# Two expert-routing stages of a macaron block on one core: gate matmul turned round, totals taken into the rank matmuls, token list and first gather moved forward

## What is computed

```python
x = L0_attn_hidden_states                      # (4, 512, 512) f32: 2048 tokens of width 512
x = x + 0.5 * ffn(layernorm(x))
x = x + attention(layernorm(x))                # 32 heads of width 16, q and k layer-normed, causal, ALiBi
x = x + 0.5 * ffn(layernorm(x))

def ffn(x, W_gate, b_gate, W_e, b_e):          # 8 experts, the same weights in both places
    logits = x @ W_gate + b_gate               # (tokens, 8)
    _, top_idx = jax.lax.top_k(logits, 2)
    y_all = relu(einsum('bsd,edh->bseh', x, W_e) + b_e)
    return take_along_axis(y_all, top_idx[..., None], axis=2).mean(axis=2)
```

## Time and profile before

| | us |
|---|---|
| median of three runs | 1024.22 |
| their range | 1021.04 to 1028.01 |
| the profiled execution, its own time | 1027.31 |
| its span in the trace | 1025.6 |
| mean granted TensorE clock | 0.921 of 2.4 GHz |

### The profile page before, as it was taken

One profiled execution on the slowest core, in us unless ns is written; L12 is line 12 of the kernel. 1 busy time (PEld: TensorE's weight loads), 2 busy tenths in 40 slices (PEclk: granted clock), 3 DMA queues, 4 the chain that ended last, 5 costly groups with the idle time before them and its releaser, 6 DMA issues. The chain is left out here.

```text
span 1025.6 us, 20208 instructions
## 1 busy us (share of the span) xinstructions
PE 873.8 (85%) x6688; PEld 646.5 (63%) x6689; DVE 638.0 (62%) x1296; ACT 444.2 (43%) x818; POOL 353.1 (34%) x342
## 2 busy tenths in 40 slices
PE   4874999992999989769999999999859993799994
PEld 4773888871777767645555555555447872688883
DVE  7955344433988877757777777777246768244441
ACT  3431333332244434527767677777623430233331
POOL 6723677763123222300000000000034420677764
PEclk9995999996999999959999999999979975799997
DMA  9954588762165599464666666562078850477863
GB/s 339 373 194 170 106 149 149 144 120 71 42 194 171 173 222 232 154 178 115 159 136 135 134 131 137 137 147 75 23 237 300 314 196 31 109 145 145 149 130 51
DMA packets 112859, 162.08 MB, mean 158 GB/s; under 512 B 16864, under 2 KB 74336, under 8 KB 112512
## 3 DMA queue, kind: packets, MB, share of 16 engines
q1 hardware_dynamic: 94928, 123.85, 41.5%
q0 software_dynamic: 17856, 37.25, 19.1%
HBM read 97.44 MB, written 67.37 MB: 161 GB/s over the span
## 5 line engine op out<-in xcount | busy, mean ns | idle before, releaser
L829 DVE TENSOR_REDUCE att_part<-att_s_ps 128x2 f32<-128x1024 f32 (+2 forms) x160 | 195.5, 1225 | 60.9 <-PE att_s_ps L677 60.5
L791 ACT ACTIVATE att_prob<-att_st_ps 128x512 f32<-128x512 f32 x320 | 173.7, 595 | 78.7 <-PE att_st_ps L703 78.6
L144 PE MATMUL exp_z_ps<-ex_w_hi,exp_xT_hi 128*128 x312 | 132.1, 423 | 1.3 <-DVE exp_xT_lo L1482 0.7
L146 PE MATMUL exp_z_ps<-ex_w_hi,exp_xT_lo 128*128 x312 | 126.2, 404 | 0.0
L145 PE MATMUL exp_z_ps<-ex_w_lo,exp_xT_hi 128*128 x312 | 125.8, 403 | 0.0
L1482 DVE TENSOR_TENSOR exp_xT_lo<-exp_t_ps,exp_xT_hi 128x512 fp32r<-128x512 f32 x78 | 54.0, 692 | 107.2 <-ACT exp_xT_hi L1468 107.2
L1475 ACT ACTIVATE exp_y<-exp_y 128x512 f32<-128x512 f32 x72 | 45.5, 632 | 168.7 <-DVE exp_y L1494 168.7
L1109 POOL TENSOR_TENSOR ex_w_lo<-ex_w_lo,ex_w_hi 128x1024 fp32r<-128x1024 f32 x32 | 76.2, 2395 | 96.2 <-ACT ex_w_hi L1213 64.9
L716 PE MATMUL att_pv_ps<-att_prob,att_v_sb 128*32 128x256 f32 (+2 forms) x1280 | 101.4, 391 | 1.8 <-ACT att_oT L796 1.8
L1410 POOL DMA_INDIRECT exp_xg<-xn,ex_token_of x78 | 78.1, 1002 | 66.2 <-SPq L1382 38.7
L641 POOL CAST att_m_parts<-att_part 128x28 fp32r<-128x28 f32 x32 | 6.6, 208 | 270.3 <-DVE att_part L833 270.3
(11 more groups left out here) (199 smaller groups left out, 1644.0 us busy)
## 6 DMA issues: line engine op xcount, KB each, us to landing
ex_w_lo<-in_L_ffn_W_e SPq DMA_DIRECT2D x32, 512.0 KB, 5.7
v_vals<-st_vals SPq DMA_DIRECT2D x16, 512.0 KB, 2.8
q_parts<-st_partq SPq DMA_DIRECT2D x32, 256.0 KB, 3.4
k_parts<-st_partk SPq DMA_DIRECT2D x32, 256.0 KB, 3.7
att_v_sb<-v_vals SPq DMA_DIRECT2D x32, 256.0 KB, 3.7
ex_bias<-in_L_attn_hidden_states SPq DMA_DIRECT2D x8, 512.0 KB, 7.8
acc<-ex_bias SPq DMA_DIRECT2D x8, 512.0 KB, 8.6
xn<-route_xn SPq DMA_DIRECT2D x8, 512.0 KB, 5.5
```

The lines of the kernel that those rows point to most:

```text
L144: nc.tensor.matmul(out, x_hi[:, s], w_hi(c), start=(c == 0), stop=False)
L146: last = nc.tensor.matmul(out, x_lo[:, s], w_hi(c), start=False, stop=(c == C - 1))
L791: nc.scalar.activation(prob[n % 2][:, col:col + 512], st_ps[(e + half) % 3][:, :], ACT.Exp).then_inc(exp_done, 1)
L829: nc.vector.tensor_reduce(out, src, X_AXIS, ALU.max, negate=True).then_inc(red_done, 1)
```

## The change

- Gate: W_gate's 128x8 blocks are the weights now and the transposed rows of both tiles of a pair (256 columns) move, four matmuls a pair into a PSUM tile of 8 partitions. xT is one tile for a pair. ACT adds the bias as it copies the 8x256 logits out (`logits_out`), and PE turns them back with two transposes (`turn_logits`). Their order on the queues is in the diff. The logits stay in PSUM, and the DVE step that added the bias is gone.
- Totals: the total is written as the rank of a seventeenth tile, so each ones matmul is 16 columns wider and the 16 small ones are gone.
- Listing: `token_of` is written directly behind `id_ps`, ahead of `expert_of`; `row_of` takes two steps fewer.
- The identity, the six small DMAs with their waits, and gather 0 are now POOL's work in the route stage. The gather waits for `token_done`, the transposes and the stores of xn. The experts' stage starts at gather 1 and waits for no identity.
- W_qkv is staged in the tile of W_out (unused in this stage) and not in `ex.bias`; the experts' bias is loaded ahead of W_qkv's third load. The last two `load_wq` waits on x are gone. ACT takes the last weights (15) one place earlier.

```diff
 class Experts
+        self.rows = m.sb("rows", [P, C, D]) if rows is None else rows
+        self.ident = m.sb("ident", [P, P])
+        self.prime = m.sb("prime", [1, ADD_RING * 16])
...
 route_block
-        w_stage = x
+        w_stage = None if w_qkv is None else [wo_turned[:, 2 * i:2 * i + 2, :] for i in range(2)]
+        xn = [ex.rows[:, 2 * i:2 * i + 2, :] for i in range(2)]
+        xT = m.sb("xT", [P, 2, C * P])
+        logits = g_ps[:, 0:TE].rearrange("p (t e) -> p t e", e=E)
+        lg_ps = route_ps if proj else wq_ps[3]
...
 SP, behind the loop
             store_xn(PAIRS - 1)
+            for i in range(XR):
+                sp.wait_ge(x_stored[i], 16 * (PAIRS // XR))
+            sp.wait_ge(xn_done, TILES)
+            sp.dma_start(ex.bias[:, :], b_e ...).then_inc(ex.bias_loaded, 16)
             if w_qkv is not None:
                 for n in range(2, WQ_PAIRS):
                     load_wq(n)
                 sp.wait_ge(wq_tr, 2 * WQ_PAIRS)
...
 POOL, ahead of the low parts
+            pool.wait_ge(ident_done, 1)
+            for r in range(ADD_RING):
+                nc.gpsimd.dma_start(ex.prime[0:1, r * 16:(r + 1) * 16], ident[0:1, 0:16]).then_inc(ex.added[r], 16)
+            for r in range(ADD_RING):
+                pool.wait_ge(ex.added[r], 16)
 POOL, behind them
+            pool.wait_ge(tr_done, TILES)
+            for par in range(2):
+                pool.wait_ge(xn_stored[par], 16 * (PAIRS // 2))
+            pool.wait_ge(token_done, 1)
+            ex.gather(nc, xn_dram, 0, ex.rows[:, 0, :])
 PE
-            def gate(t):
-                pe.wait_ge(copied, t + 1)
+            def gate(u):
+                pe.wait_ge(copied, 2 * u + 2)
+                at_least(pe, lg_out, u)
                 for c in range(C):
-                    last = nc.tensor.matmul(g_ps[:, t * E:(t + 1) * E], xT[t % 2][:, c * P:(c + 1) * P], g_raw[:, c, :],
+                    last = nc.tensor.matmul(lg_ps[0:E, 0:2 * P], g_raw[:, c, :], xT[:, :, c * P:(c + 1) * P],
                                             start=(c == 0), stop=(c == C - 1))
+            def turn_logits(u):
+                pe.wait_ge(lg_out, u + 1)
+                for k in range(2):
+                    t = 2 * u + k
+                    last = nc.tensor.transpose(g_ps[:, t * E:(t + 1) * E], lgT[:, k * P:(k + 1) * P], ident[0:E, 0:E])
+                last.then_inc(gate_done, 1)
             for u in range(PAIRS + 2):
                 if u >= 2:
-                    gate(2 * u - 4)
-                    gate(2 * u - 3)
+                    gate(u - 2)
...
                     transpose(2 * u - 1)
+                if u >= 2:
+                    turn_logits(u - 2)
...
+            nc.tensor.matmul(total_ps, ones_bf[:, :], both[:, 0:2 * E], start=False, stop=False, skip_group_check=True)
             for s in range(1, TILES):
-                last = nc.tensor.matmul(rank_ps[:, s * 2 * E:TE2], ones_bf[:, :], both[:, 0:TE2 - s * 2 * E], start=False,
-            for s in range(TILES):
-                last = nc.tensor.matmul(total_ps, ones_bf[:, :], both[:, s * 2 * E:(s + 1) * 2 * E],
+                last = nc.tensor.matmul(route_ps[:, s * 2 * E:TE2 + 2 * E], ones_bf[:, :], both[:, 0:TE2 - (s - 1) * 2 * E],
 ACT
             def copy(t):
-                at_least(act, gate_done, t - 1)
+                at_least(act, lg_done, t // 2)
+            def logits_out(u):
+                act.wait_ge(lg_done, u + 1)
+                at_least(act, gate_done, u)
+                nc.scalar.activation(lgT, lg_ps[0:E, 0:2 * P], ACT.Identity, bias=bg[:, 0:1]).then_inc(lg_out, 1)
...
                     o_split(2 * u + 3)
+                if u >= 2:
+                    logits_out(u - 2)
                 if u >= 1:
                     copy(2 * u - 2)
                     copy(2 * u - 1)
-                if u < PAIRS - 1:
+                if u < PAIRS:
                     weights(2 * u + 1)
-            weights(TILES - 1)
+            logits_out(PAIRS - 1)
 DVE, behind the 32 one-hots
+            dve.wait_ge(ids_done, 2 * TILES)
+            chain(nc.vector.tensor_copy(found[:, :, :], ids))
+            nc.vector.scalar_tensor_tensor(ex.token_of[:, :], found[:, 2, :], float(P), found[:, 1, :],
+                                           ALU.mult, ALU.add).then_inc(token_done, 1)
             chain(nc.vector.tensor_tensor(past[:, :, :], ends[0:1, :] ...
...
 expert_block, POOL
-            gather(0)
-            make_identity(nc, pool, ident, zeroed, ident_done)
             for s in range(1, AHEAD):
                 gather(s)
-            pool.wait_ge(ident_done, 1)
-            for r in range(RING):
-                nc.gpsimd.dma_start(prime[0:1, r * 16:(r + 1) * 16], ident[0:1, 0:16]).then_inc(added[r], 16)
-            for r in range(RING):
-                pool.wait_ge(added[r], 16)
```

More of the change, by code:

```diff
@@ L865, with __init__ @@
 class Experts:
-    def __init__(self, nc, ctx, prefix):
+    def __init__(self, nc, ctx, prefix, rows=None):
         m = Memory(nc, ctx, prefix)
+        self.rows = m.sb("rows", [P, C, D]) if rows is None else rows
+        self.ident = m.sb("ident", [P, P])
+        self.prime = m.sb("prime", [1, ADD_RING * 16])
+        self.gathered = [m.sem(f"gathered{i}") for i in range(ADD_RING)]
+        self.added = [m.sem(f"added{i}") for i in range(ADD_RING)]
         self.w_hi = m.sb("w_hi", [P, E * C, D], F32R)
@@ L881, in __init__, with gather @@
         self.bias_loaded = m.sem("bias_loaded")
+    def gather(self, nc, xn_dram, s, xg):
+        nc.gpsimd.indirect_dma_start(out=xg, out_offset=None, in_=xn_dram[:, :],
+                                     in_offset=bass.IndirectOffsetOnAxis(ap=self.token_of[:, s:s + 1], axis=0)
+                                     ).then_inc(self.gathered[s % ADD_RING], 16)
 def ring_loop(engine, step, total, ring, first):
@@ L954, in route_block @@
         rest = work[:, TE:2 * TE].rearrange("p (t e) -> p t e", e=E)
+        logits = g_ps[:, 0:TE].rearrange("p (t e) -> p t e", e=E)
+        lg_ps = route_ps if proj else wq_ps[3]
+        lgT = work[0:E, 0:2 * P]
+        root = m.sb("root", [P, 4])[:, :] if proj else route_ps[:, 0:4]
         slot_e = work[:, :].rearrange("p (t k e) -> p t k e", k=2, e=E)
@@ L1076, in _ @@
                 sp.wait_ge(wq_tr, 2 * WQ_PAIRS)
-            for i in range(XR):
-                sp.wait_ge(x_stored[i], 16 * (PAIRS // XR))
-            sp.wait_ge(xn_done, TILES)
-            sp.dma_start(ex.bias[:, :], b_e.rearrange("(a e) h -> a (e h)", a=1).to_broadcast([P, E * D])).then_inc(ex.bias_loaded, 16)
-            sp.wait_ge(bias_loaded, 16)
             for par in range(2):
@@ L1294, in _ @@
             dve.wait_ge(const_done, 12)
-            dve.wait_ge(bias_loaded, 16)
-            dve.wait_ge(gate_done, TILES)
+            dve.wait_ge(gate_done, PAIRS)
             three = [P, TILES, E]
-            chain(nc.vector.tensor_tensor(logits[:, :, :], g_ps[:, 0:TE].rearrange("p (t e) -> p t e", e=E),
-                                          bg_bc[:, :].rearrange("p (a e) -> p a e", a=1).to_broadcast(three), ALU.add))
             for k, source in enumerate((logits, rest)):
@@ L1385, in expert_block @@
         AHEAD = RING - 1
-        ident = m.sb("ident", [P, P])
-        xg = [m.sb(f"xg{i}", [P, D]) for i in range(RING)]
+        ident = ex.ident
+        xg = [ex.rows[:, i, :] if i < C else m.sb(f"xg{i}", [P, D])[:, :] for i in range(RING)]
         xT_hi = [m.sb(f"xT_hi{i}", [P, C * P], F32R) for i in range(2)]
@@ L1393, in expert_block @@
         z_ps = [m.ps(f"z_ps{i}") for i in range(2)]
-        zeroed, ident_done = m.sem("zeroed"), m.sem("ident_done")
-        gathered = [m.sem(f"gathered{i}") for i in range(RING)]
-        added = [m.sem(f"added{i}") for i in range(RING)]
+        gathered, added = ex.gathered, ex.added
         tr_done, hi_done, lo_done, z_done, zb_done, y_done = (
```

57 lines of the change are left out of this document (24 added, 33 removed).

## The result

The changed kernel takes 1031.62 us in the median of 20 runs (1029.01 to 1035.55), the kernel before 1026.43 in the median of 20. The ratio is 1.0044, with a 95% interval of 1.0027 to 1.0062. So the change costs 4.5 us by the ratio (2.8 to 6.4) and 5.2 by the medians, where the forecast had a gain of 5.6; 1031.62 lies above the range's end of 1027.5. Of the 13.0 us between 1031.62 and the forecast's 1018.6, 2.2 come from its base, the median of three runs (1024.22 for 1026.43). The profiled execution took 1029.65 us, with a span of 1027.9.

What follows compares the result with a forecast made beforehand. Bound by the engine-to-engine routing chain, and by PE in route 2's loop. Route 1 (0 - 0.3 - 4.0) and route 2 (+2.5 - 1.3 - 0.3 - 2.2) gave -5.6 us: 1018.6 from 1024.22, range 1009.5 to 1027.5.

Steps and rivals of the forecast that it cites:

- Gate, what is new on the path: Gate start, route 2's loop: waiting for both copies behind `logits_out` starts it 0.8 to 0.9 us later; +4.7 us over six gates.
- The six small DMAs move to a POOL that is idle: POOL, route stage: moving them there costs nothing, or up to 1 us of shift in a stage bound elsewhere.
- Gate's own time: PE's eight gate matmuls per pair: 1.8 us at full speed, bounds 0.9 and 2.1, hardly changed from 1.95.
- the cheap gate of 0.9: Lower bound of PE's gate time per pair, from half an fp32r matmul of 512 columns: 0.9 us.
- The loop of route 2: Route 2's pairs: later gate starts +4.7 us, removed clock drops -2.2; together +2.5 us (-2.2 to +6.9).
- Gate in route 1: Last pair of route 1: +2.7 us at half clock, -1.9 at full speed; taken as 0, first reduction near 65.8.
- Listing and gather: Listing to first expert matmul: earlier `token_of` and gather 0 gain 4.0 us in route 1, 2.2 in route 2.
- The slower rival: Route 2's loop and both last pairs: the gate makes PE's pair longer; +4.3 us, 1028.5 us, chance 0.15.
- the likeliest case: The forecast itself, whole kernel: PE's gate pair at 1.8 us, total -5.6 us, 1018.6 us, chance 0.50.
- The rival of the clock: Both routes: the clock stays up and the wide gate is cheap; -14.1 us, 1010.1 us, chance 0.25.
- The start that isn't carried: Experts' stages: POOL holds their end where it is despite the earlier start; +0.6 us, 1024.8 us, chance 0.10.
- if the stages of qkv and attention differ by more than 1 us: Stages of qkv and attention: a difference above 1 us was named as showing the forecast wrong.

Runs made afterwards that it cites:

- the priming DMAs alone: Kernel before with only the six small DMAs and their waits moved from the experts' stage to POOL's idle time in the route stage: 1.0024 of the kernel before.
- the other kernel: Kernel before with one edit, the scratch of the reciprocal root moved to SBUF in route 2: 1.0076 of the kernel before.

## Why the prediction was wrong

By the ratios, the changed kernel with the scratch back in PSUM is at 0.9996, and with POOL's DMAs back too at 0.9958 and 0.9962. So the change is three things: 4.9 us lost by the scratch, 3.7 us lost by where POOL's DMAs stand, 4.1 us gained by the rest; each of the three leaves 2 to 3 us open either way. The forecast of -5.6 described the rest and had no term for the other two.

- **The step that failed first** is the one under "Gate, what is new on the path", which priced the copies, `logits_out` and `turn_logits`, and not what had to leave the bank that the new logits took. It measured 3.3 us in route 2's loop by the timelines, 4.9 us by the ratios, whose intervals leave 2.6 us open either way.
- **The second** is "The six small DMAs move to a POOL that is idle ... nothing, or up to 1 us". They lengthen the end of each experts' stage by 2.3 us, by the DRAIN (4.15 to 6.43, the priming DMAs alone), and the kernel before by 2.5 us in all (0.2 to 4.7). The sum treated the end of POOL's stage as the last add.
- **Gate's own time**: right. 1.89 us at full speed for 1.8; the cheap gate of 0.9 is out.
- **The loop of route 2**: the steady pair right in every part. Gates 10.47 us apart for 10.4, PE idle 0.67 us ahead of the gate and 0.16 ahead of `turn_logits`, no pair below clock 1.00. Timeline of one pair:

```profile
816.48 0.45 ACT L1249 ACTIVATE route_work<-route_route_ps,route_bg 8x256 f32<-8x256 f32 x1
816.84 1.05 ACT L1242 ACTIVATE route_xT<-route_t_ps 128x512 f32<-128x512 f32 x2
816.98 0.29 PE L1179 MATMUL route_g_ps<-ex_ident,route_work 8*128 8x8 f32 x2 [0.16 <-ACT route_work L1249]
...
817.94 1.89 PE L1171 MATMUL route_route_ps<-route_xT,route_g_raw 128*8 128x256 f32 x8 [0.67 <-ACT route_xT L1242]
```

  With the scratch in PSUM first gate to first reduction is 69.39 us for 69.56, where the sum had +2.5 - 1.3 = +1.2: the drops of the clock gave back more than was put down. The sum read the second slow window of the earlier trace rows wrongly. It took 10.26 us as 0.6 more than a pair at 1.00, but that window has 49 matmuls and not 56. With the narrow gate, the new order of ACT and the clock at 1.00 it is 8.69 us, so the drop cost about 1.6. Window of the kernel with the old gate in route 2:

```profile
820.77:829.46 8.69, 8.44 (x49) 7.15 (x49) 8.14 (x20) 2.98 (x5) 4.93 (x2) 1.00 0.34 140
```

  In the changed kernel first gate to first reduction was +3.3, and all of the excess over the 69.39 is the scratch.
- **Gate in route 1**: 0 was taken. The first reduction comes at 61.1 to 66.2 us in the twelve kernels with the wide gate there and at 63.0 to 65.8 in the five with the narrow one: no difference beyond this scatter.
- **Listing and gather**: the mechanism was right, its size too large. The sum had 4.0 us in route 1 and 2.2 in route 2 from the listing to the first expert matmul; from the end of DVE's last step to that matmul it measured 9.78 to 6.32 (3.5) and 7.65 to 6.12 (1.5). What was missed is a DRAIN again: gather 0 holds GpSimd's closing DRAIN of the route stage back (3.87 us from 86.48 to 90.35, for 2.45 hidden behind DVE), so that it ends 1.06 us behind DVE's last step, and gather 1 is issued 1.95 us behind that step, where the sum had 1.2 (91.6 to 92.8). With gather 0 back in the experts' stage that DRAIN is hidden again, and the start is only 1.2 us later than in the changed kernel. Timeline of the kernel with all of POOL's DMAs back, route 2:

```profile
866.98 0.19 DVE L1405 SCALAR_TENSOR_TENSOR ex_before_of<-route_begin_f,route_n_ring 1x40 int32<-1x40 f32 x1
868.42 1.06 POOL L890 DMA_INDIRECT wo_turned<-xn,ex_token_of  x1 [19.03 <-SPq L1411]
869.78 0.97 POOL L890 DMA_INDIRECT wo_turned<-xn,ex_token_of  x1 [0.31 <-issue]
...
873.40 1.13 PE L1467 MATMUL exp_t_ps<-ex_ident,wo_turned 128*128 128x128 f32 x4 [0.43 <-DMA wo_turned<-xn,ex_token_of]
```

  The first expert matmul comes 7.3 us behind DVE's last step here (874.48 less 867.17), for 6.1. An early gather 0 buys about 1.2 us in this stage and 1.0 to 1.1 in route 1. The listing needs no early gather: `token_of` comes 21.74 us behind the first reduction here, for 24.55 before, in both routes.
- **The slower rival** forecast 1028.5 by a dearer pair of PE. It came slower, but not by that mechanism: PE's pair was as in the likeliest case.
- **The rival of the clock** fell with the gate at 1.89 us; its other half, a clock of 1.00 all through route 2, came true. **The start that isn't carried** is neither shown nor excluded: from the first expert matmul to the last add it is 137.0 and 138.4 us before, 138.4 and 139.7 in the changed kernel, 136.8 and 140.4 in the kernel with both repairs. The changed kernel is 1.4 and 1.3 us longer than the one before, and the repaired one 0.2 shorter and 2.0 longer: that scatter is as large as the effect.
- **The sign "if the stages of qkv and attention differ by more than 1 us"** came, and the sum had nothing for it. Between the DRAINs of their stages qkv takes 191.1 us before and 190.2 in the changed kernel, attention 287.0 and 289.0. Attention takes 286.7 to 289.0 us over all the kernels here, so this is taken for scatter, 1.1 us in sum; it is not shown to be more.
- W_qkv's staging and the totals were not tried alone. From the first reduction to DVE's last step it is 25.7 us before and 25.2 to 25.4 with the new totals and list, for the 0.3 less of the sum.

## What to carry to other kernels

When a new tile takes a PSUM bank, ask who used that bank and where that data goes. A scratch that moves to SBUF can turn a free step into one that waits for GpSimd; look for steps of one shape whose time jumps from 0.16 to 2.3 us, and read the busy time of an engine that the change gives nothing to do. The end of a stage is not its last transfer: with a barrier the closing instruction of each engine counts, and work moved off a path can lengthen it.

With the repairs (scratch in PSUM, POOL's DMAs in the experts' stage) the rest of the change is worth about 4 us over the kernel before (1.8 to 6.8 by the widest interval), with either gate; the simplest such version keeps the old gate.

## What was not expected of the hardware

- DVE with two SBUF inputs waits out a GpSimd subtraction that reads SBUF (2.32 beside 2.37 us, 2.20 to the same end in the other kernel); with the scratch in PSUM each of the 88 small steps of route 2 is 0.16 to 0.17 us, in each of eleven kernels. In the six with it in SBUF these steps take 14 to 17 us more in sum. Two SBUF inputs are not the whole condition. A small step with one input waits at times too, as the first pair of rows shows (changed kernel: both end at 767.6), and so does the normalisation, which has one tensor in SBUF (second pair, changed kernel with the scratch back: 2.62 us beside 2.59).

```profile
765.21 2.36 POOL L1128 TENSOR_TENSOR ex_w_lo<-ex_w_lo,ex_w_hi 128x1024 fp32r<-128x1024 f32 x1 [0.21 <-ACT ex_w_hi L1253]
765.98 1.62 DVE L82 TENSOR_SCALAR route_root<-route_mv 128x2 f32<-128x2 f32 x1
...
828.50 2.59 POOL L1128 TENSOR_TENSOR ex_w_lo<-ex_w_lo,ex_w_hi 128x1024 fp32r<-128x1024 f32 x1
828.75 2.62 DVE L1331 TENSOR_SCALAR wo_turned<-ex_bias,route_mv,route_rstd 128x512 f32<-128x512 f32 x1
```

- GpSimd's closing DRAIN of a stage with 77 to 94 DMAs takes 4.15 to 6.93 us though POOL has waited for the last of them, and one DMA more (85 for 84) moved it by 2.4 us. In the route stage it is 2.44 us without DMAs and 2.95 with six small ones early, again 0.08 us for each, but 3.8 to 3.9 with gather 0 at its end, with or without the six.
- In every timed kernel with the wide gate route 2's steady pairs stood at clock 1.00; with the narrow one each kernel had one to three of its first six windows at 0.83 to 0.87. The gain is eaten by the gate's own gap: 68.16 against 69.38 us.
